# One set of logits for two softmaxes: raw logits kept in DRAM, shifted by GpSimd, transposed by TensorE

## Chip, cores, metric

One Trainium2 chip, one of its cores. The metric is the device time of one launch in microseconds; lower is better. Engines are called TensorE (PE in the profile, PEld for its weight loads), VectorE (DVE), ScalarE (ACT), GpSimd (POOL) and SyncE (SP, which only issues DMAs). "q" behind an engine's name is its sequencer.

## What is computed

Eight batch elements of 256 tokens x 128 channels go through four residual layers, all in float32. The change touches the third layer's mixture of slots (64 experts with 32 slots each, 2048 columns). Both softmaxes are taken of the same logits: D over the 32 slots of an expert, C over the 64 experts of a slot.

```python
logits = (jnp.einsum('tzd,ed->tze', x, phi_w) + phi_b).reshape(t, z, n, p)   # t=8, z=256, n=64, p=32
D = jax.nn.softmax(logits, axis=3)
C = jax.nn.softmax(logits, axis=2)
X_tilde = jnp.einsum('tznp,tzd->npd', D, x)          # summed over all batch elements
X_tilde = tanh(layer_norm(clip(X_tilde)))
Y_tilde = jnp.einsum('npd,ndH->npH', X_tilde, expert_w) + expert_b[:, None, :]
Y = jnp.einsum('tznp,npH->tzH', C, Y_tilde)
```

X_tilde needs D of all eight elements before Y of the first can be made: so the layer has a join in its middle. The layer before it (a mixture of MLPs and skills) makes u, the x of these lines. The fourth layer is a linear attention input, 16-head attention and a routed feed-forward.

## The kernel before

The kernel works in stages. Stage A holds layer 1 and half of layer 2. Stage B holds, for each batch element b, the end of layer 2 (BC, Z, LN, ZN, ZT, X2), the skills (SG, SU, UC, UT) and the D side of the slots (LG, MT, SH, XT, MC). Then comes the join (JC, JR, JB, JT, JX, JN, JM, JA: norm, tanh, the experts' products). Stage D holds the C side (CL, CSA, CSB, CSUM, REC, CN, Y, X3) and layer 4 (S, V, Q, K, RQ, RK, QM, MX, NM, TS, AV, AVT, SAT, WO, X5, G3, GE, FF, SO, RT, FIN, OUT, ST).

The order on each engine is written out by hand as a string of steps, NAME.b, in ORDER_BD (stages B to D) and ORDER_A. Each engine runs its own string in that order, so a step whose semaphore has not come holds all that stand behind it on its engine. Steps of several batch elements are mixed, so that stage B of b+1 runs beside that of b. PSUM is two halves of four banks: low (the skills, later CL and layer 4) and high (the logits, later the attention scores).

D side, per batch element, in eight steps of 512 columns (four of 1024: half h of the columns and half k of the tokens, each in two parts c). TensorE makes LG in a bank of high (L1021, f32, and L1022, the bias in three bf16 parts). VectorE reduces it over slots (L1822), splits the negated maxima in two bf16 parts (L1824, L1826), and reduces over experts (L1827). TensorE transposes the maxima (MT, L1029), ScalarE copies them (L1406), TensorE adds them to the bank with a selection matrix (SH, L1033), and ScalarE takes exp of it (L1411). VectorE sums (L1834) and scales (L1838); XT (L1046) multiplies by u and VectorE adds to xacc (L1847). MC joins the maxima over experts (L1852) and leaves them transposed in mcR.

C side, per batch element. TensorE makes the logits again, transposed, in eight steps CL of two 128-column tiles (L1104), with maxima and bias from mcR and selPx (L1105). ScalarE takes exp into eC (L1438). GpSimd adds quarters of eC (CSA L2118, CSB L2123), VectorE adds the rest (CSUM, L1894 to L1898), TensorE folds it over partitions (L1111), VectorE takes the reciprocal (REC, L1901) and scales eC in four steps (CN, L1907). Y (L1118) multiplies by the experts' outputs in four steps. X3 (L1910) adds it to x.

Other names: W and WA on GpSimd make weights of layer 4 (L2098, L2101), RSZ the norm's power for ZN (L2080, L2082); JR the same for the join. L1766 to L1773 on VectorE pick the tokens of layer 2 and scale the mask that BC.0 waits for. EWA and EWB load expert weights, EBD the biases and layer 4's weights (18 loads).

## Time and profile before

| | us |
|---|---|
| median of 3 runs | 1195.12 |
| lowest, highest | 1194.73, 1200.56 |
| the profiled execution | 1194.49 |
| its span, first to last instruction | 1192.6 |

| engine | busy us | share of the span | instructions |
|---|---|---|---|
| TensorE | 1032.1 | 87% | 6734 |
| VectorE | 765.5 | 64% | 1829 |
| ScalarE | 518.0 | 43% | 836 |
| GpSimd | 158.1 | 13% | 166 |

The rows below are of the profiled execution, which took 1.9 us more than its span. Busy times of TensorE are those of a pipelined engine: a listed duration holds the way through the array, and the next instruction starts before it ends, so starts are to be compared for its rate. A share over the whole span is an average over stages with different limits.

### The profile page before, as it was taken

What the parts mean: (1) busy time and instruction counts of PE and PEld (TensorE: products, weight loads), DVE (VectorE), ACT (ScalarE), POOL (GpSimd) and SP (SyncE); (2) the same over time, 40 slices, a digit from 0 to 9 for tenths busy, and PEclk for the clock granted to TensorE, in tenths of its full rate; (3) what the DMA queues carried; (4) which work ended last, traced back from release to release, by engine and by line L of the source; (5) the groups of instructions that cost most, each with busy time, mean ns of one, the idle gap of its engine ahead of it and who ended that gap; (6) DMA issues with size and microseconds to landing.
All of it is one profiled execution on the core that took longest, in us unless ns stands there. A gap on an engine that the chain in (4) does not pass through costs nothing.

```text
span 1192.6 us, 18208 instructions
## 1 busy us (share of the span) xinstructions
PE 1032.1 (87%) x6734; PEld 765.7 (64%) x6760; DVE 765.5 (64%) x1829; ACT 518.0 (43%) x836; POOL 158.1 (13%) x166
## 2 busy tenths in 40 slices
PE   3989999998648899999999953788999999998755
PEld 2878888886436667776766733566666666666432
DVE  4565555554574678888888777536567676676432
ACT  1245445435322554465557312235455536543510
POOL 1120110100307300000000004201212022011000
PEclk9999999999768999999999987999999999999976
DMA  8010000000300221001300003000000000000000
GB/s 319 2 28 15 14 15 14 14 14 2 124 0 1 85 93 54 17 38 53 124 1 1 1 1 107 1 1 1 1 6 1 6 1 5 6 1 6 5 5 5
DMA packets 11800, 35.39 MB, mean 30 GB/s; under 512 B 2570, under 2 KB 5818, under 8 KB 10944
## 3 DMA queue, kind: packets, MB, share of 16 engines
q1 hardware_dynamic: 10464, 33.14, 7.8%
q8 instruction: 54, 0.88, 0.3%
q10 hardware_dynamic: 1152, 1.05, 0.3%
q14 instruction: 34, 0.28, 0.1%
q0 software_dynamic: 96, 0.04, 0.0%
HBM read 33.16 MB, written 1.06 MB: 29 GB/s over the span
## 4 chain that ended last, share of the span: by engine, by line
PE 58%; issue 18%; DVE 15%; DVEq 4%; ACT 2%; POOL 1%; POOLq 1%; another core or an unknown queue 0%; ACTq 0%
PE ps L1118 5%; PE ps L1104 5%; PE ps L836 5%; PE ps L1001 3%; PE ps L1046 3%; PE ps L1258 3%; PE ps L1179 3%; PE ps L1159 2%; DVE arena L1822 2%; PE ps L1197 2%; PE ps L870 2%; PE ps L1021 2%; PE ps L846 2%; PE ps L882 2%; PE ps L994 2%
## 5 line engine op out<-in xcount | busy, mean ns | idle before, releaser
L1926 DVE TENSOR_REDUCE arena<-ps 128x8 f32<-128x2048 f32 x32 | 73.3, 2291 | 37.3 <-PE ps L1159 37.3
L1465 ACT ACTIVATE arena<-ps 128x2048 f32<-128x2048 f32 x32 | 60.1, 1879 | 57.5 <-PE ps L1183 57.5
L1104 PE MATMUL ps<-uR,arena 128*128 128x256 f32 x256 | 74.6, 386 | 0.1
L1258 PE MATMUL ps<-arena 128*128 128x512 f32 x128 | 68.2, 657 | 5.5 <-DVE xacc L2000 4.4
L1021 PE MATMUL ps<-arena,uR 128*128 128x512 f32 x128 | 67.7, 610 | 3.5 <-ACT arena L1411 3.0
L1046 PE MATMUL ps<-arena 128*128 128x128 f32 x512 | 64.9, 281 | 6.7 <-DVE arena L1838 5.0
L1046 PEld LDWEIGHTS ps<-arena 128*128 128x128 f32 x512 | 62.4, 196 | 12.1 <-issue 7.9
L1118 PE MATMUL ps<-arena 128*128 128x256 f32 x256 | 63.9, 395 | 6.6 <-DVE arena L1907 3.7
L1438 ACT ACTIVATE arena<-ps 128x512 f32<-128x512 f32 x64 | 38.0, 598 | 60.5 <-PE ps L1105 54.1
L1118 PEld LDWEIGHTS ps<-arena 128*128 128x128 f32 x256 | 47.9, 194 | 20.0 <-issue 9.6
L836 PE MATMUL ps<-arena 128*128 128x256 f32 x256 | 58.0, 384 | 0.0
L994 PE MATMUL ps<-x2R,arena 128*128 128x256 f32 x192 | 52.0, 394 | 5.6 <-DVE arena L1813 5.4
L1822 DVE TENSOR_REDUCE arena<-ps 128x16 f32<-128x512 f32 x64 | 44.3, 692 | 17.7 <-remote 7.9
L836 PEld LDWEIGHTS ps<-arena 128*128 128x128 f32 x256 | 49.2, 193 | 7.3
L986 PE MATMUL ps<-x2R,arena 128*128 128x256 f32 x192 | 51.0, 388 | 0.9 <-ACT arena L1392 0.4
L1411 ACT ACTIVATE arena<-ps 128x512 f32<-128x512 f32 x64 | 38.2, 598 | 29.7 <-PE ps L1033 28.5
L1104 PEld LDWEIGHTS ps<-uR,arena 128*128 128x128 f32 x256 | 39.6, 190 | 16.7 <-issue 5.2
L994 PEld LDWEIGHTS ps<-x2R,arena 128*128 128x128 f32 x192 | 35.0, 193 | 18.3 <-DVE arena L1813 12.9
L1001 PE MATMUL ps<-arena 128*128 128x256 f32 x192 | 43.3, 380 | 3.5 <-DVE arena L1813 3.5
L1258 PEld LDWEIGHTS ps<-arena 128*128 128x128 f32 x128 | 23.5, 201 | 33.5 <-issue 20.0
L1179 PE MATMUL ps<-arena,x1C 32*128 32x256 f32 x512 | 41.3, 409 | 3.4 <-ACT arena L1465 3.3
L1827 DVE TENSOR_REDUCE arena<-ps 128x32 f32<-128x512 f32 x64 | 43.8, 684 | 0.2 <-issue 0.2
(381 smaller groups left out, 2355.5 us busy)
## 6 DMA issues: line engine op xcount, KB each, us to landing
arena<-in_skills SPq DMA_DIRECT2D x16, 768.0 KB, 5.7
arena<-in_expert_w SPq DMA_DIRECT2D x2, 2048.0 KB, 8.3
arena<-in_l_experts SPq DMA_DIRECT2D x8, 386.5 KB, 3.1
arena<-in_consts_b SPq DMA_DIRECT2D x1, 1152.0 KB, 9.5
x2R<-in_x ACTq DMA_DIRECT2D x8, 128.0 KB, 6.5
arena<-in_L_w SPq DMA_DIRECT2D x2, 512.0 KB, 12.1
arena<-in_phiC SPq DMA_DIRECT2D x1, 1024.0 KB, 12.6
arena<-in_expert_b SPq DMA_DIRECT2D x1, 1024.0 KB, 4.9
```

The source lines that it names most:

```text
L836: last = mm(mid[:, j * T:(j + 1) * T], w0[w][:, e, :], S8a[u][:, e, :], start=e == 0, stop=e == E - 1)
L994: last = mm(low[:, 3, j * T:(j + 1) * T], w[:, 4 + 2 * h + j, :], x2R[:, b, :], start=True, stop=True)
L1001: last = mm(low[:, 2, 0:T], w[:, 8 + j, :], H3[u][:, 4 * m + j, :], start=m == 0 and j == 0, stop=m == 2 and j == 3)
L1021: mm(high[:, c, :], uR[:, b, k * P:(k + 1) * P], phiC[:, col:col + 512], start=True, stop=False)
L1046: last = mm(high[:, 2, t * P:(t + 1) * P], eD[h][:, k, col:col + P], uT[u][:, k, :], start=k == 0, stop=k == 1)
L1104: mm(o, phiC[:, st_ * P:(st_ + 1) * P], uR[:, b, :], start=True, stop=False)
L1118: last = mm(low[:, 1, 0:T], ytl[:, t, :], eC[u][:, t, :], start=t == 0, stop=t == ST - 1)
L1179: mm(scores[:, c, h * T:(h + 1) * T], kR[u][row, t * P:(t + 1) * P], qm[u][row, g, :], start=True, stop=False)
L1258: last = mm(low[:, 3, :], pm[:, 2 + j, k * P:(k + 1) * P], w2e[:, j, c * 512:(c + 1) * 512], start=j == 0, stop=j == 1)
L1465: av(pexp[:, t, gp].rearrange("p c h t -> p (c h t)"), scores[:, :, :].rearrange("p c t -> p (c t)"), ACT.Exp, scale=SCALE3).then_inc(s.sc ...
L1822: V.tensor_reduce(nmd, lg, X, ALU.max, negate=True)
L1926: V.tensor_reduce(nm[:, k, :, 2 * gp:2 * gp + 2], scores[:, :, :].rearrange("p c (h t) -> p c h t", h=2), X, ALU.max, negate=True).then_in ...
```

## The change

The logits are made once per batch element. LG writes to one of three banks of high in turn, ScalarE copies it raw to SBUF (LC, new; raw[j], four tiles of 1024 columns, where stage B's hid was), and VectorE takes both maxima from there, four steps LG instead of eight (nmd over slots, nmc over experts). GpSimd adds the slot maxima (DS, new), ScalarE takes exp in place (SH, four of 1024). MT, the SH products and MC's transpose go; MC is one minimum. SyncE stores each raw tile to DRAM (KP, 512 KB each).

For the C side SyncE reads 2 MB per element back (BACK: tokens on partitions, double buffer cT). GpSimd adds the expert maxima (CM, two of 2048), ScalarE takes exp (CE, two of 2048), VectorE sums over the 64 experts in one reduction per half (CB, reading 32 words apart), takes the reciprocal of 64 sums and spreads it over 256 columns (REC). TensorE transposes these (CR) and the 16 tiles of both halves (TC, eight steps of four transposes in place of CL), VectorE copies CR's result (RC) and scales each TC step from PSUM into eC (CN, eight steps of 512), which is now one buffer; Y waits for all CN. CSA, CSB, CSUM, selPx, mcR and three constants go. EWA, EWB and EBD wait for other things, and ORDER_BD is written anew for all engines. The arena grows from 35396 to 37240 words.

In the diff a line of three dots stands where lines are left out, most of the removed ones among them.

```diff
 ORDER_BD = {
     "SP": """
-    LOAD.0 LOAD.1 LOAD.2 EWA.0 LOAD.3 LOAD.4 LOAD.5 LOAD.6 EWB.0 LOAD.7 EBD.0 ST.0 ST.1 ST.2 ST.3 ST.4 ST.5 ST.6
-    ST.7""",
+    LOAD.0 LOAD.1 LOAD.2 KP0.0 KP1.0 KP2.0 KP3.0 LOAD.3 KP0.1 KP1.1 KP2.1 KP3.1 LOAD.4 KP0.2 KP1.2 KP2.2 KP3.2 LOAD.5
+    KP0.3 KP1.3 KP2.3 KP3.3 LOAD.6 KP0.4 KP1.4 KP2.4 KP3.4 LOAD.7 KP0.5 KP1.5 KP2.5 KP3.5 EWA.0 KP0.6 KP1.6 KP2.6
+    KP3.6 BACK.0 KP0.7 KP1.7 KP2.7 KP3.7 EWB.0 BACK.1 EBD.0 BACK.2 BACK.3 BACK.4 BACK.5 ST.0 BACK.6 ST.1 BACK.7 ST.2
+    ST.3 ST.4 ST.5 ST.6 ST.7""",
     "ACT": """
...
+    UC.7 SH3.6 UT.7 LC0.7 LC1.7 LC2.7 CE0.0 LC3.7 LC4.7 SH0.7 LC5.7 LC6.7 CE1.0 LC7.7 SH1.7 SH2.7 SH3.7 CE0.1 CE1.1
+    JT0.0 JT1.0 JN0.0 JN1.0 CE0.2 CE1.2 S.0 V.0 NM.0 CE0.3 TS0.0 CE1.3 TS1.0 S.1 TS2.0 V.1 AV0.0 TS3.0 AV1.0 CE0.4
...
     "DVE": """
...
+    SH2.6 SH3.6 LG0.7 XT1.6 CB0.0 SH0.7 XT2.6 LG1.7 XT3.6 LG2.7 LG3.7 SH1.7 MC.7 CB1.0 XT0.7 XT1.7 SH2.7 SH3.7 REC.0
+    XT2.7 JC0.0 RC.0 XT3.7 JC1.0 JB0.0 CN0.0 CN1.0 JB1.0 CN2.0 CN3.0 CN4.0 CN5.0 CB0.1 CN6.0 CN7.0 CB1.1 REC.1 JA0.0
+    JA1.0 CB0.2 CB1.2 X3.0 RQ.0 RC.1 RK.0 CN0.1 CN1.1 MX0.0 CN2.1 CN3.1 MX1.0 CN4.1 CN5.1 MX2.0 CN6.1 CN7.1 MX3.0 NM.0
+    REC.2 CB0.3 X3.1 CB1.3 RQ.1 RK.1 RC.2 REC.3 CN0.2 CN1.2 MX0.1 CN2.2 CN3.2 MX1.1 CN4.2 CN5.2 MX2.1 CN6.2 CN7.2
...
     "POOL": """
-    W.0 WA.0 W.1 RSZ.0 WA.1 W.2 WA.2 W.3 RSZ.1 WA.3 W.4 WA.4 W.5 WA.5 RSZ.2 W.6 WA.6 W.7 WA.7 RSZ.3 RSZ.4 RSZ.5
...
+    W.0 W.1 WA.1 W.2 WA.2 W.3 WA.3 W.4 WA.4 W.5 WA.5 W.6 WA.6 W.7 WA.7 RSZ.0 RSZ.1 RSZ.2 DS0.0 DS1.0 RSZ.3 DS2.0 DS3.0
+    DS0.1 DS1.1 DS2.1 DS3.1 DS0.2 RSZ.4 DS1.2 DS2.2 DS3.2 DS0.3 DS1.3 RSZ.5 DS2.3 DS3.3 RSZ.6 DS0.4 DS1.4 DS2.4 RSZ.7
+    DS3.4 DS0.5 DS1.5 DS2.5 DS3.5 DS0.6 DS1.6 DS2.6 DS3.6 CM0.0 DS0.7 CM1.0 DS1.7 DS2.7 DS3.7 CM0.1 CM1.1 JR0.0 VZ.0
+    JR1.0 CM0.2 CM1.2 QM.0 CM0.3 CM1.3 QM.1 CM0.4 CM1.4 RS1.0 QM.2 CM0.5 CM1.5 RS1.1 QM.3 RS2.0 CM0.6 CM1.6 RS1.2
+    RS2.1 QM.4 CM0.7 CM1.7 RS1.3 QM.5 RS2.2 RS1.4 QM.6 RS2.3 RS1.5 QM.7 RS2.4 RS1.6 RS2.5 RS1.7 RS2.6 RS2.7""",
...
+                for j in range(4):
+                    if n == f"KP{j}":
+                        sp.wait_ge(s.raw_copied, at(b, 8, 2 * j + 1))
+                        sp.dma_start(raw_d[b, j // 2, j % 2], raw[j]).then_inc(kept[j], 16)
...
+                if n == "EWB":
+                    sp.wait_ge(s.max_ready, 8 * NB)
+                    sp.wait_ge(s.shifted, 4 * NB)
+                    for j in range(4):
+                        sp.wait_ge(kept[j], 16 * NB)
+                    sp.dma_start(ew_c[1], A["expert_w"][1]).then_inc(s.ew_loaded, 16)
...
+                if n == "BACK":
+                    if b == 0:
+                        sp.wait_ge(s.uC_mm, NB)
+                    if b == 1:
+                        sp.wait_ge(s.lg_mm, 8 * NB)
+                    if b >= 2:
+                        sp.wait_ge(s.tc_mm, at(b - 2, 9, 8))
+                    for j in range(4):
+                        sp.wait_ge(kept[j], 16 * at(b))
+                    for k in range(K):
+                        sp.dma_start(cT[u][k].rearrange("p (h c) -> p h c", h=2),
+                                     raw_d[b, :, k].rearrange("h p c -> p h c")).then_inc(raw_back[u], 16)
...
+                        if i >= 3:
+                            pe.wait_ge(s.raw_copied, i - 2)
                         col = h * HALF + c * 512
...
+                        bank = high[:, LG_BANK[i % 3], :]
+                        mm(bank, uR[:, b, k * P:(k + 1) * P], phiC[:, col:col + 512], start=True, stop=False)
+                        mm(bank, ones_rows, phib3[:, col:col + 512], start=False, stop=True).then_inc(s.lg_mm, 1)
...
+                if n == "CR":
+                    pe.wait_ge(s.csum_ready, at(b, 3, 2))
+                    if b == 0:
+                        pe.wait_ge(s.zn_ready, NB)
+                        pe.wait_ge(s.zn_aff, NB)
+                    else:
+                        pe.wait_ge(s.rope_done, at(b - 1, 4, 0))
+                    for k in range(K):
+                        last = tr(low[:, 0, k * P:(k + 1) * P], rsum[:, k * P:(k + 1) * P], ident)
+                    last.then_inc(s.tc_mm, 1)
+                if n[:2] == "TC":
                     a = int(n[2:])
                     if a == 0:
...
+                        pe.wait_ge(s.eC_ready, at(b, 9, 0))
+                        pe.wait_ge(s.c_exp, at(b, 2, 1))
+                    elif a == 1:
                         if b > 0:
...
+                            pe.wait_ge(s.rope_done, at(b - 1, 4, 2))
                     else:
...
+                        pe.wait_ge(s.eC_ready, at(b, 9, a - 1))
                     for t in range(2):
...
+                        for k in range(K):
+                            st_ = 2 * a + t
+                            last = tr(low[:, a % 2, t * T + k * P:t * T + (k + 1) * P], cT[u][k][:, st_ * P:(st_ + 1) * P], ident)
+                    last.then_inc(s.tc_mm, 1)
...
+                    if n == f"LC{st_}":
+                        act.wait_ge(s.lg_mm, at(b, 8, st_))
+                        if c == 0:
+                            if b == 0:
+                                act.wait_ge(s.z_mm, at(j))
+                            else:
+                                act.wait_ge(s.max_ready, at(b - 1, 8, 2 * j + 1))
+                                act.wait_ge(s.shifted, at(b - 1, 4, j))
+                                act.wait_ge(kept[j], 16 * b)
+                        av(raw[j][:, c * 512:(c + 1) * 512], high[:, LG_BANK[i % 3], :], ACT.Copy).then_inc(s.raw_copied, 1)
+                for j in range(4):
+                    if n == f"SH{j}":
+                        act.wait_ge(s.shifted, at(b, 4, j))
+                        av(eD[j // 2][:, j % 2, :], eD[j // 2][:, j % 2, :], ACT.Exp).then_inc(s.eD_ready, 1)
...
+                    if n == f"CE{k}":
+                        act.wait_ge(s.c_shifted, at(b, 2, k))
+                        av(cT[u][k], cT[u][k], ACT.Exp).then_inc(s.c_exp, 1)
...
+                    if n == f"LG{j}":
                         dr()
...
+                        dve.wait_ge(s.raw_copied, at(b, 8, 2 * j + 1))
+                        if 4 * b + j >= 2:
+                            dve.wait_ge(s.shifted, 4 * b + j - 1)
+                        lg = raw[j].rearrange("p (n q) -> p n q", q=PSLOT)
+                        V.tensor_reduce(nmd[j % 2], lg, X, ALU.max, negate=True).then_inc(s.max_ready, 1)
+                        V.tensor_reduce(nmc[:, k, h, :], lg.rearrange("p n q -> p q n"), X, ALU.max,
+                                        negate=True).then_inc(s.max_ready, 1)
...
+                    V.tensor_tensor(mcA[:, b, :].rearrange("p (k q) -> p k q", k=K), nmc[:, :, 0, :], nmc[:, :, 1, :],
+                                    ALU.min).then_inc(s.mc_ready, 1)
...
+                    if n == f"CB{k}":
+                        dr()
+                        dve.wait_ge(s.c_exp, at(b, 2, k))
+                        V.reduce_sum(csum[:, k * PSLOT:(k + 1) * PSLOT], cT[u][k].rearrange("p (n q) -> p q n", q=PSLOT),
+                                     X).then_inc(s.csum_ready, 1)
                 if n == "REC":
...
+                    dr()
+                    V.reciprocal(csum, csum)
+                    dr()
+                    if b > 0:
+                        dve.wait_ge(s.tc_mm, at(b - 1, 9, 0))
+                    V.tensor_copy(rsum.rearrange("p (k r q) -> p k r q", k=K, r=4),
+                                  csum.rearrange("p (k q) -> p k q", k=K).unsqueeze(2).to_broadcast([P, K, 4, PSLOT])).then_inc(s.csum_ready, 1)
+                if n == "RC":
+                    dve.wait_ge(s.tc_mm, at(b, 9, 0))
+                    V.tensor_copy(rC, low[:, 0, 0:T]).then_inc(s.eC_ready, 1)
+                if n[:2] == "CN":
+                    a = int(n[2:])
+                    dve.wait_ge(s.tc_mm, at(b, 9, a + 1))
+                    if a == 0:
                         dr()
...
+                        if b == 0:
+                            dve.wait_ge(s.uC_mm, NB)
+                        else:
+                            dve.wait_ge(s.Y_mm, at(b - 1))
+                    V.tensor_tensor(eC[:, 2 * a:2 * a + 2, :], low[:, a % 2, :].rearrange("p (t c) -> p t c", t=2),
+                                    rC.unsqueeze(1).to_broadcast([P, 2, T]), ALU.mult).then_inc(s.eC_ready, 1)
...
+                    if n == f"DS{j}":
+                        pool.wait_ge(s.max_ready, at(b, 8, 2 * j))
+                        if b > 0:
+                            pool.wait_ge(s.xt_mm, at(b - 1, 4, 2 * h + 1))
+                        tile = [P, 32, PSLOT]
+                        G.tensor_tensor(eD[h][:, k, :].rearrange("p (n q) -> p n q", q=PSLOT),
+                                        raw[j].rearrange("p (n q) -> p n q", q=PSLOT),
+                                        nmd[j % 2].unsqueeze(2).to_broadcast(tile), ALU.add).then_inc(s.shifted, 1)
...
+                    if n == f"CM{k}":
+                        pool.wait_ge(raw_back[u], 32 * (b // 2 + 1))
+                        pool.wait_ge(s.mc_ready, at(b))
+                        c = cT[u][k].rearrange("p (n q) -> p n q", q=PSLOT)
+                        G.tensor_tensor(c, c, mcA[:, b, k * PSLOT:(k + 1) * PSLOT].unsqueeze(1).to_broadcast([P, NSLOT, PSLOT]),
+                                        ALU.add).then_inc(s.c_shifted, 1)
```

## Rows read from the trace of the kernel before

**Rows 1.** Busy table: stretch, length, busy us (PE, PEld, DVE, ACT, POOL), PEclk, DMA

```profile
460.00:660.00 200.00, 189.90 (x1000) 143.06 (x1016) 171.18 (x321) 113.16 (x173) 3.37 (x7) 1.00 0.12 43
...
660.00:717.00 57.00, 43.24 (x233) 30.06 (x236) 42.54 (x76) 15.63 (x35) 0.30 (x2) 0.94 0.00 1
...
826.00:1070.00 244.00, 241.76 (x1955) 162.15 (x1954) 162.99 (x293) 131.04 (x187) 41.48 (x33) 1.00 0.01 3
```

**Rows 2.** Chain of waits from 742 us on: start us, us, what

```profile
825.80 1.83 PE ps L1118 x8
...
1070.15 1.73 PE ps L1118 x8
```

**Rows 3.** Groups by form, stage B: line, operation, count | busy us, mean ns | idle

```profile
L1822 DVE TENSOR_REDUCE arena<-ps 128x16 f32<-128x512 f32 x64 | 44.3, 692 | 17.7 <-remote 7.9 <-PE ps L1022 5.0 <-issue 1.0
...
L1824 DVE CAST arena<-arena 128x16 bf16<-128x16 f32 x64 | 12.4, 193 | 5.0 <-issue 0.4
...
L1827 DVE TENSOR_REDUCE arena<-ps 128x32 f32<-128x512 f32 x64 | 43.8, 684 | 0.2 <-issue 0.2
...
L1834 DVE TENSOR_REDUCE arena<-arena 128x32 f32<-128x1024 f32 x32 | 38.7, 1211 | 0.6 <-ACT arena L1411 0.5
...
L1852 DVE TENSOR_REDUCE arena<-arena 128x64 f32<-128x256 f32 x8 | 4.8, 596 | 0.8
```

**Rows 4.** Order of time on TensorE: start us, us, engine, line, operation

```profile
894.23 0.60 PE L1207 MATMUL ps<-cst,arena 128*128 128x128 f32 x4
...
912.18 0.59 PE L1104 MATMUL ps<-uR,arena 128*128 128x256 f32 x2
...
912.62 0.28 PE L1105 MATMUL ps<-mcR,selPx 67*128 67x256 bf16 x1
...
912.73 0.60 PE L1104 MATMUL ps<-uR,arena 128*128 128x256 f32 x2
```

**Rows 5.** Groups by form, stage D

```profile
L1901 DVE RECIPROCAL y1C<-ps 128x256 f32<-128x256 f32 x8 | 14.0, 1754 | 3.7 <-PE ps L1111 3.6
...
L1907 DVE TENSOR_TENSOR arena<-arena,y1C 128x1024 f32<-128x1024 f32 x32 | 38.4, 1220 | 0.6
...
L1894 DVE TENSOR_TENSOR arena<-w3raw,arena 128x1024 f32<-128x1024 f32 x8 | 9.8, 1225 | 4.7 <-ACT arena L1438 4.5 <-POOL w3raw L2123 0.2
...
L1465 ACT ACTIVATE arena<-ps 128x2048 f32<-128x2048 f32 x32 | 60.1, 1879 | 57.5 <-PE ps L1183 57.5
...
L1438 ACT ACTIVATE arena<-ps 128x512 f32<-128x512 f32 x64 | 38.0, 598 | 60.5 <-PE ps L1105 54.1 <-PE ps L1001 6.1
```

**Rows 6.** Order of time on GpSimd and VectorE where both work

```profile
328.60 1.91 POOL L2098 TENSOR_TENSOR arena<-w3raw,condc 128x1024 f32<-128x1024 f32 x1
...
328.81 1.98 DVE L1754 TENSOR_TENSOR arena<-arena 128x256 f32<-128x256 f32 x1
...
330.87 0.43 DVE L1756 TENSOR_TENSOR arena<-arena 128x256 f32<-128x256 f32 x1
...
375.78 2.35 POOL L2101 TENSOR_TENSOR wb<-wb,arena 128x1024 f32<-128x1024 f32 x1 [0.16 <-issue]
...
377.48 0.75 DVE L1813 SCALAR_TENSOR_TENSOR arena<-ps,wsel,arena 128x512 f32<-128x512 f32 x1 [0.65 <-PE ps L994]
...
393.27 2.15 DVE L1805 TENSOR_TENSOR x2R<-x2R,sqC 128x256 f32<-128x256 f32 x1 [3.98 <-ACT sqC L1385]
```

**Rows 7.** Order of time on VectorE at the start of stage B

```profile
350.85 0.29 DVE L1770 TENSOR_SCALAR arena<-arena 128x256 f32<-128x256 f32 x1
...
351.23 2.19 DVE L1773 TENSOR_SCALAR arena<-arena,cst 128x256 bf16<-128x256 f32 x8
```

**Rows 8.** Order of time on VectorE around the join

```profile
716.73 0.82 DVE L1864 TENSOR_SCALAR xacc<-xacc 128x1024 f32<-128x1024 f32 x1
...
749.05 0.42 DVE L1910 TENSOR_TENSOR x2R<-x2R,ps 128x256 f32<-128x256 f32 x1 [7.35 <-PE ps L1118]
```

**Rows 9.** DMA issues: count, KB each, median us to landing

```profile
arena<-in_expert_w SPq DMA_DIRECT2D x2, 2048.0 KB, 8.3
```

386 lines of the change are left out of this document (122 added, 264 removed).

## Prediction

> **What bounds the kernel now.** I read the busy table by stretch first, then the grouped instructions, then the order of time on single engines. [rows 1] In the steady part of the middle stage (460 to 660 us, called stage B) TensorE is busy 189.9 us of 200 and VectorE 171.2 of 200, with 321 VectorE instructions and their short gaps filling most of the rest: two engines are full together. From 660 to 717 us, where the last batches have no TensorE work left to overlap, VectorE is busy 42.5 of 57 us. In the last stage (stage D, 826 to 1070) TensorE is busy 241.8 of 244 and VectorE 163.0: TensorE bounds it. [rows 2] give the first quarter of the Y product of batches 2 and 7 (825.80 and 1070.15), so five batches take 244.35 us, 48.9 each. GpSimd works 41 us of those 244 and 3.4 us of the 200 in stage B: it is the free engine that the change loads.
>
> **The change, part by part.**
>
> Stage B, TensorE. Per batch eight MT transposes and eight SH products go. A bf16 product of 256 columns advances the queue by 0.11 us (912.62 to 912.73 [rows 4]), so SH of 512 costs 0.22, eight are 1.8 us; an MT, of 64 columns, is below the 0.11 of that row, some 0.5 for eight. TensorE saves some 2.3 us of 39 per batch, 18 in all.
>
> Stage B, VectorE. Now each half tile costs two reductions, 0.692 and 0.684 us, and two short conversions near 0.19 [rows 3]: 64 x 1.75 = 112 us. After it each of 32 tiles of 1024 columns costs a contiguous maximum, 1.211 (as L1834 does), and one over the experts, which steps 32 words in SBUF. The nearest row for that is L1852: 256 elements, same step, 0.598 us. L1822 and L1834 differ by 0.52 us for 512 elements, so contiguous reading costs 1.01 ns an element and 0.17 us for the instruction; L1852 leaves 1.66 ns an element. The maximum over experts is then 0.17 + 1024 x 1.66 ns = 1.87 us, and 32 x 3.08 = 99 us: 13 less. MC falls from 0.6 + two conversions to one short operation: 6 less. Fewer instructions in a chain save about 4 us of gaps. Together -23. Bounds for the strided maximum: 1.21 (contiguous) to 1.87, since both are rows.
>
> What it adds there: the two strided sums of batch 0 are put before the join of the stages, at 0.17 + 2048 x 1.66 ns = 3.57 us each, and a reciprocal and a copy of 64 to 256 elements: +8.
>
> GpSimd's holds. DS adds four GpSimd operations of 1024 elements per batch. Rows for such operations run from 1.91 to 2.35 us [rows 6]. They hold VectorE: at 328.81 a 256-element operation that takes 0.43 elsewhere (330.87) took 1.98, ending 0.28 after GpSimd's at 330.51. At 377.48 an operation with one input in PSUM ran 0.75 us inside a GpSimd operation (375.78 to 378.13) as ever. So those with both inputs in SBUF wait. Stage B has six of these per batch (four SH multiplies, X2, MC). GpSimd would be busy 9.4 us of 38, a quarter; a hold met at random costs half its 2.35: 48 x 0.25 x 1.2 = 14 us. GpSimd also waits on VectorE and DS falls mostly beside the reductions, so I take +10 (0 to 28, all meeting one). The Trainium skill, "SBUF — State Buffer", section "SBUF: two separate sides", says that a GpSimd operation and a VectorE one with two SBUF inputs (or in a two-port mode) exclude each other for the whole instruction, and others are not held. The two rows agree, and by that rule the strided maxima, with one input, run free and the sum stays as below. No row has such a maximum inside a GpSimd operation; were it held too, all 32 x 2.35 = 75 us of DS could fall on VectorE, and the sum would end 65 later.
>
> Stage B together: -23 + 8 + 10 = -5, between TensorE's own -18 and +13.
>
> The end of stage B. SP loads BACK.0 (2 MB) only after the last UC; GpSimd has CM0.0 in front of DS0.7 in its queue, so all of batch 7's DS wait behind that load and a 2048-element CM. A 2 MB load lands in 8.3 us [rows 9]; CM is two of the 1.91 to 2.35 us operations, 4.2. DS0.7 could start some 5 us after UC.7 and starts after 12.5; VectorE has 3 to 4 us of other work there. +4 (0 to 8).
>
> The start of stage B. Today's order stops GpSimd after W.1 until statistics come; the new one runs all W and WA at once, 13 operations of about 2.2 us, to about 360 us. VectorE still has three two-input or two-port operations before its top-k loop, then the nine scalings of L1770 and L1773 that TensorE's BC.0 waits for [rows 7]. Three holds of about 1.9 net are 5.6 us; the loop itself (one data input) ends at 356 then, and its followers meet the last W: 3 more. Back comes what those W cost later, as at 393.27 (2.15 for a 0.43 operation [rows 6]): -3. Net +6 (0 to 12).
>
> The join. JR0.0 (the norm's power, GpSimd) now stands behind CM0.1 and CM1.1, and JT0.0 (tanh, ScalarE) behind CE1.1; both need BACK.1, issued behind a 2 MB EWB that itself waits for the last DS. Two such loads are 14 to 16 us from the last DS, the two CM 8.4. X3.0 on VectorE stands behind CB1.2, which needs BACK.2, issued after the 18 loads of EBD. Today JC.0 to X3.0 is 32.7 us (716.73 to 749.05, and its 0.42 [rows 8]). Followed through the new queues, counted from JC.0: TC.0 ends near 17, BACK.2 lands at 25.5, CM 30 and 34, CE 36, CB1.2 40, X3.0 after it: +7 (0 to 14, the lower end where the loads land early).
>
> Stage D, TensorE. A CL step is two pairs of 0.44 + 0.11 (912.18, 912.62, 912.73): 1.10 us. A TC step is four f32 128x128 transposes: listed with 0.60 us for four, and as a listed duration overruns the advance by 0.17 (0.28 for 0.11 at 912.62), 0.11 each, 0.44 [rows 4]. 8 x 0.66 = 5.3 us per batch less; CSUM's product is replaced by two transposes, about 0.2 less.
>
> Stage D, VectorE. Out: CSUM (1.22 and, by size, 0.69 and 0.43), REC 1.75, four CN of 1.22 [rows 5]: 9.0. In: two sums 7.1, reciprocal and copies 1.2, eight CN from PSUM at 0.7 (as the 0.75 of 377.48 for 512 columns): 13.9. 163.0/5 = 32.6 becomes 37.5, with gaps about 40.5. CM holds GpSimd's side 8.4 us per batch instead of CSA and CSB's 4.3; few D operations have two SBUF inputs, and the four CN and CSUM that had leave: +1. TensorE needs 48.9 - 5.5 = 43.4 if nothing else moved. With VectorE at 41.5 in order beside it I expect 45.5, -3.4 x 6 batch steps = -20 (-32 if TensorE alone sets it, +4 if VectorE does at 49.5). ScalarE and the DMA queues hide: CE is 2 x 1.88 against CL's 8 x 0.6 [rows 5], and 2 MB in and 2 MB out per batch are 17 us of DMA in 39 or 48; without that cover each would show as waits of CM or LC.
>
> Sum on the profiled execution, 1194.49 us (span 1192.6): +6 - 5 + 4 + 7 - 20 = -8, so 1186. The median of the runs shown is 1195.12, 0.6 more.
>
> **The rivals.**
>
> TensorE keeps its whole saving: the holds and the join cost little, B gives 18, D 32, the start 6 back: 1194.5 - 44 = 1150. For it: TensorE is the fullest engine in both stages. Against: VectorE is as full in B, and grows in D.
>
> Nothing shows: D gives half (-10), the queues' new positions eat it: 1189 to 1201. For it: four waits on BACK lie on chains that nothing covers.
>
> Slower: GpSimd holds VectorE. Where DS and the six two-input operations fall together always (one waits for the other's result through ScalarE, so they keep step), B loses 30 instead of 10 and D's holds take 5 us per batch: VectorE 45, step 48: -1 x 6. +6 + 15 + 4 + 7 - 6 = +26, 1220. It decides from about 18 us of holds in B with D at -12. For it: 1.98 for 0.43. Against: the operations with PSUM inputs run free.
>
> **How the numbers follow.** Forecast 0.42 (its own range 1176 to 1196), TensorE alone 0.18, nothing 0.15, slower by holds 0.25. 0.5% is 6 us, about what a measurement of this kernel can tell from none. Faster than 1189: all of the first rival and most of the forecast's lower part, 0.48; within 1189 to 1201: 0.23; slower 0.29. Two in ten left out: 1153 to 1216.
>
> **What would show it.** The sums over experts at 3.6 us and the maxima at 1.9 (2.3 and 1.2 would refute L1852 as the model). TC steps 0.44 apart. Y's quarters 45.5 us apart. X2, SH's multiply and MC lengthened where DS runs. BC.0 starting 9 us later. VectorE idle before CB0.0, CB1.2. Wrong: steps of D at 48 or more, or a join longer by over 14 us.

## The result, and the profile after

The changed kernel takes 1228.61 us (median of 4, 1223.07 to 1236.55), the kernel before beside it 1197.05. The ratio is 1.0266 with a 95% interval of 1.0202 to 1.0331: 2 to 3% slower, where 1186 was forecast. The profiled execution took 1236.55 us with a span of 1234.8, the longest of the four; stretches below are of it, so their sum, 42.2 us, is some 11 more than the difference of the medians. Of run e8 below, one of five executions, the profiled one (1162.48 us), was in a slower state of the chip, so its time here is the median of the other four.

First where the time lies. From the order of time on TensorE I took when the first instruction of a step starts (end: the last instruction of the span). The last column is the fastest kernel of the experiments (e14 below: the changed kernel with its steps in another order and one GpSimd instruction cut in four).

| from, to | before, us | after, us | difference | forecast | e14, us |
|---|---|---|---|---|---|
| start to UC.0 | 386.9 | 390.9 | +4.0 | +6 | 377.8 |
| UC.0 to UC.7 (stage B) | 270.6 | 290.9 | +20.3 | -5 | 253.5 |
| UC.7 to the end of XT.7 | 58.4 | 68.9 | +10.5 | +4 | 62.7 |
| end of XT.7 to Y.0 | 25.9 | 25.4 | -0.5 | | 21.8 |
| Y.0 to OUT.0 | 143.7 | 155.0 | +11.3 | +7 with the row above | 136.0 |
| OUT.0 to the end | 307.0 | 303.7 | -3.3 | -20 | 277.3 |
| whole span (rows rounded singly) | 1192.6 | 1234.8 | +42.2 | -8 | 1129.0 |

The busy table of the changed kernel, in the columns and for the stretches of [rows 1]; the last line is its own stage B:

```profile
460.00:660.00 200.00, 173.94 (x862) 134.98 (x872) 155.67 (x181) 86.99 (x115) 39.85 (x27) 0.94 0.23 90
660.00:717.00 57.00, 42.95 (x200) 30.19 (x201) 47.17 (x43) 23.26 (x32) 20.98 (x9) 0.95 0.28 111
826.00:1070.00 244.00, 214.39 (x1775) 147.06 (x1776) 178.54 (x294) 94.39 (x131) 48.37 (x29) 0.93 0.10 37
390.90:681.80 290.90, 255.07 (x1238) 194.20 (x1251) 217.06 (x256) 126.85 (x172) 55.03 (x38) 0.95 0.23 91
```

and stage B of the kernel before (386.90 on) and of e14 (377.80 on):

```profile
386.90:657.50 270.60, 254.04 (x1323) 189.82 (x1345) 223.48 (x419) 152.86 (x232) 14.66 (x17) 1.00 0.14 51
```

```profile
377.80:631.30 253.50, 241.71 (x1247) 183.40 (x1247) 216.33 (x255) 141.80 (x185) 75.24 (x47) 0.99 0.28 102
```

What to see: in [rows 1] TensorE and VectorE were both nearly full; after, neither is. In stage B TensorE idles 290.9 - 255.1 = 35.8 us instead of 16.6 (+19.2), and its mean granted clock is 0.95 instead of 1.00, which by estimate is 0.05 x 290.9 = 14.5 us of full-speed work not granted (somewhat less, since a part of the low clock fell in idle time). Without those 14.5 its work is some 240.6 us against 254.0 (-13.4): the work did shrink. +19.2 + 14.5 - 13.4 = 20.3. VectorE has 6.4 us less work and also waits more. The e14 line has the same instructions, GpSimd's cut one apart, with TensorE idle 11.8 us: the saving is there once the order lets it be.

The waits of stage B that engines spent on each other, after (engine, line, waited for: us, times, longest; L997 is SU, L1797 the instruction of VectorE it needs, L1037 is XT, L1828 VectorE's addition of it):

```profile
PEld ps L997 <- DVE arena L1797: 20.5, 19, 4.0
DVE xacc L1828 <- PE ps L1037: 20.3, 11, 3.8
...
PE ps L997 <- DVE arena L1797: 11.7, 9, 3.6
...
PE ps L1037 <- DVE xacc L1828: 9.1, 3, 4.5
```

TensorE waits for VectorE and VectorE for TensorE, in turn. In the kernel before the first three of these pairs are 12.5, 7.3 and 5.4 us in stage B and the fourth does not occur there; in e14 the four are 12.7, 2.9, 5.7 and 0.7 us.

The groups that answer to [rows 3] and [rows 5], by form:

```profile
L1806 DVE TENSOR_REDUCE arena<-arena 128x32 f32<-128x1024 f32 x32 | 39.0, 1220 | 11.8 <-ACT arena L1398 7.9 <-issue 3.4 <-POOL arena L2063 0.3
L1807 DVE TENSOR_REDUCE arena<-arena 128x32 f32<-128x1024 f32 x32 | 61.8, 1931 | 0.0
...
L1868 DVE TENSOR_REDUCE arena<-arena 128x32 f32<-128x2048 f32 x16 | 58.8, 3676 | 33.9 <-ACT arena L1422 32.9
...
L1890 DVE TENSOR_TENSOR arena<-ps,y1C 128x512 f32<-128x512 f32 x64 | 41.5, 685 | 6.2 <-PE ps L1093 5.0
...
L2063 POOL TENSOR_TENSOR arena<-arena 128x1024 f32<-128x1024 f32 x32 | 60.9, 1904 | 213.1 <-DVE arena L1806 186.1 <-PE ps L1037 27.0
...
L2102 POOL TENSOR_TENSOR arena<-arena,mcA 128x2048 f32<-128x2048 f32 x16 | 64.5, 4053 | 140.7 <-DMA arena<-raw_scratch 140.7
```

These are the two maxima of LG, the sum CB, the scaling CN, and GpSimd's DS and CM. Each lies within 4% of the forecast's size (1.21, 1.87, 3.57, 0.7; DS at the lower end of 1.91 to 2.35; CM 4.2). New is the last figure of L1868: VectorE stood still 32.9 us in front of the sums, waiting for ScalarE's exp of them.

The Y product, first quarter of batches 2 and 7 (order of time on TensorE), for [rows 2]:

```profile
850.23 1.57 PE L1102 MATMUL ps<-arena 128*128 128x256 f32 x6
...
1091.37 1.90 PE L1102 MATMUL ps<-arena 128*128 128x256 f32 x8
```

241.1 us for five batches, 48.2 each against 48.9: of TensorE's 5.5 us per batch, 0.7 appeared.

### The profile page after: what moved, and what is told of

Its sections match the earlier page's. It is cut to its first block, busy times and chain, and to the rows that moved or that the text cites. A ratio compares the mean times of both kernels' runs of the same rounds, so it can differ in the third digit from the quotient of the medians.

```text
span 1234.8 us, 17278 instructions
## 1 busy us (share of the span) xinstructions
PE 1003.0 (81%) x6473; PEld 756.4 (61%) x6488; DVE 804.1 (65%) x1661; ACT 462.8 (37%) x700; POOL 239.2 (19%) x192
## 4 chain that ended last, share of the span: by engine, by line
PE 37%; issue 33%; DVE 11%; POOL 8%; DVEq 4%; ACT 4%; POOLq 3%; ACTq 0%; another core or an unknown queue 0%
PE ps L840 5%; POOL arena L2102 4%; PE ps L997 2%; PE ps L1037 2%; PE ps L989 2%; PE ps L886 2%; PE ps L874 2%; PE ps L1242 2%; DVE arena L1815 2%; PE ps L850 2%; PE ps L897 2%; POOLq L2078 2%; DVE arena L1868 1%; PE ps L1102 1%; DVE arena L1819 1%
## 5 line engine op out<-in xcount | busy, mean ns | idle before, releaser
L1037 PE MATMUL ps<-arena 128*128 128x128 f32 x512 | 76.0, 311 | 44.2 <-DVE arena L1819 25.3
L1037 PEld LDWEIGHTS ps<-arena 128*128 128x128 f32 x512 | 72.2, 222 | 52.4 <-issue 35.6
L2063 POOL TENSOR_TENSOR arena<-arena 128x1024 f32<-128x1024 f32 x32 | 60.9, 1904 | 213.1 <-DVE arena L1806 186.1
L2102 POOL TENSOR_TENSOR arena<-arena,mcA 128x2048 f32<-128x2048 f32 x16 | 64.5, 4053 | 140.7 <-DMA arena<-raw_scratch 140.7
L1910 DVE TENSOR_REDUCE arena<-ps 128x8 f32<-128x2048 f32 x32 | 73.2, 2288 | 13.8 <-PE ps L1143 13.4
L1868 DVE TENSOR_REDUCE arena<-arena 128x32 f32<-128x2048 f32 x16 | 58.8, 3676 | 33.9 <-ACT arena L1422 32.9
L1102 PE MATMUL ps<-arena 128*128 128x256 f32 x256 | 63.0, 394 | 5.9 <-DVE arena L1855 5.8
L997 PE MATMUL ps<-x2R,arena 128*128 128x256 f32 x192 | 54.2, 407 | 12.9 <-DVE arena L1797 12.5
L1422 ACT ACTIVATE arena<-arena 128x2048 f32<-128x2048 f32 x16 | 30.6, 1910 | 86.3 <-POOL arena L2102 86.2
L1807 DVE TENSOR_REDUCE arena<-arena 128x32 f32<-128x1024 f32 x32 | 61.8, 1931 | 0.0
L1102 PEld LDWEIGHTS ps<-arena 128*128 128x128 f32 x256 | 49.4, 199 | 16.4 <-issue 8.9
L840 PE MATMUL ps<-arena 128*128 128x256 f32 x256 | 59.4, 391 | 0.0
L1402 ACT ACTIVATE arena<-arena 128x1024 f32<-128x1024 f32 x32 | 33.8, 1057 | 60.2 <-POOL arena L2063 60.0
L840 PEld LDWEIGHTS ps<-arena 128*128 128x128 f32 x256 | 50.2, 197 | 7.6
L1376 ACT ACTIVATE arena<-ps 128x512 f32<-128x512 f32 x48 | 28.7, 598 | 66.4 <-PE ps L989 66.1
L1398 ACT ACTIVATE arena<-ps 128x512 f32<-128x512 f32 x64 | 37.8, 595 | 42.2 <-PE ps L1025 26.4
L997 PEld LDWEIGHTS ps<-x2R,arena 128*128 128x128 f32 x192 | 35.7, 198 | 28.0 <-DVE arena L1797 22.8
L1163 PE MATMUL ps<-arena,x1C 32*128 32x256 f32 x512 | 43.7, 429 | 10.3 <-ACT arena L1448 7.0
## 6 DMA issues: line engine op xcount, KB each, us to landing
arena<-in_L_w SPq DMA_DIRECT2D x2, 512.0 KB, 10.5
```

Of the source, the lines that this page charges most:

```text
L840: last = mm(mid[:, j * T:(j + 1) * T], w0[w][:, e, :], S8a[u][:, e, :], start=e == 0, stop=e == E - 1)
L997: last = mm(low[:, 3, j * T:(j + 1) * T], w[:, 4 + 2 * h + j, :], x2R[:, b, :], start=True, stop=True)
L1037: last = mm(high[:, 2, t * P:(t + 1) * P], eD[h][:, k, col:col + P], uT[u][:, k, :], start=k == 0, stop=k == 1)
L1102: last = mm(low[:, 1, 0:T], ytl[:, t, :], eC[:, t, :], start=t == 0, stop=t == ST - 1)
L1807: V.tensor_reduce(nmc[:, k, h, :], lg.rearrange("p n q -> p q n"), X, ALU.max, negate=True).then_inc(s.max_ready, 1)
L1868: V.reduce_sum(csum[:, k * PSLOT:(k + 1) * PSLOT], cT[u][k].rearrange("p (n q) -> p q n", q=PSLOT), X).then_inc(s.csum_ready, 1)
```

## The experiments

All times are medians; "to before" is the ratio to the kernel before on the same chip, with its 95% interval. The changed kernel itself is 1.0266 (1.0202 to 1.0331).

| run | what | us | to before |
|---|---|---|---|
| e1 | maximum over a quarter of the experts | 1217.89 | 1.0219 (1.0179 to 1.0259) |
| e2 | sum over a quarter of the experts | 1217.44 | 1.0186 (1.0165 to 1.0207) |
| e3 | DS on a quarter of the columns | 1226.01 | 1.0279 (1.0249 to 1.0308) |
| e4 | raw logits of one element stored | 1229.71 | 1.0282 (1.0255 to 1.0309) |
| e6 | sums later in VectorE's queue | 1238.85 | 1.0344 (1.0288 to 1.0400) |
| e7 | steps of the D side reordered | 1187.55 | 0.9931 (0.9909 to 0.9953) |
| e8 | all steps of stages B to D reordered | 1148.35 | 0.9601 (0.9560 to 0.9643) |
| e9 | the kernel before, reordered likewise | 1176.48 | 0.9827 (0.9789 to 0.9865) |
| e10 | e8 by a second search | 1155.15 | 0.9680 (0.9663 to 0.9696) |
| e11 | e9 by the second search | 1198.22 | 1.0034 (1.0021 to 1.0046) |
| e12 | e6, with CM in four pieces | 1214.05 | 1.0172 (1.0153 to 1.0191) |
| e13 | halving on GpSimd, then VectorE's sum | 1249.39 | 1.0467 (1.0433 to 1.0502) |
| e14 | e8, with CM in four pieces | 1132.02 | 0.9472 (0.9426 to 0.9518) |
| e15 | after, with CM in four pieces | 1230.86 | 1.0287 (1.0219 to 1.0355) |

### Is it the new work itself? (e1 to e4)

e1 takes three quarters of the strided maximum away:

```diff
-  V.tensor_reduce(nmc[:, k, h, :], lg.rearrange("p n q -> p q n"), X, ALU.max, negate=True)
+  V.tensor_reduce(nmc[:, k, h, :], lg[:, 0:8, :].rearrange("p n q -> p q n"), X, ALU.max, negate=True)
...
```

> The changed kernel, with the maximum over the experts taken over 8 of a tile's 32 experts (three quarters of that reduction are left out). The changed kernel takes 1228.6. In its trace such a reduction takes 1.93 us; with a quarter of the elements it should take about 0.6, so VectorE loses 32 x 1.33 = 43 us of work, 40 of them before the join. If VectorE's amount of work sets the time of stage B, 1190 to 1200. If stage B is set by the chain from one engine to the next (slot maximum, GpSimd's addition, exp, sum) and by gaps in fixed orders, only what stands in a chain comes back: 1212 to 1222. If GpSimd holds VectorE, 1228: this operation has one input and was not lengthened.

```profile
L1807 DVE TENSOR_REDUCE arena<-arena 128x32 f32<-128x256 f32 x32 | 18.9, 589 | 0.0
```

and its stage B, in the columns of [rows 1]:

```profile
389.80:664.40 274.60, 243.65 (x1237) 186.17 (x1250) 187.41 (x256) 126.41 (x171) 55.02 (x38) 0.99 0.25 96
```

VectorE lost 61.8 - 18.9 = 43 us of work, 30 of them in the stage in which it was thought to bound, and the kernel 11 us by the medians (6 by the ratios). Stage B took 274.6 us in this one trace, where it took 290.8 to 290.9 in those of the changed kernel and of e2, e4, e6, e13 and e15, which leave it alone. So VectorE's work has a part in it; but TensorE's idle time fell by 4.9 us only (35.8 to 31.0), most of the rest is its clock (0.99 instead of 0.95), and the four waits above still are 16.7, 18.0, 9.6 and 8.8 us. With 36 us less VectorE work in it than the kernel before, the stage is still 4 us longer than there. e2 does the same to the sum:

```diff
-  V.reduce_sum(csum[...], cT[u][k].rearrange("p (n q) -> p q n", q=PSLOT), X)
+  V.reduce_sum(csum[...], cT[u][k][:, 0:16 * PSLOT].rearrange("p (n q) -> p q n", q=PSLOT), X)
```

> The changed kernel, with the sum over the experts taken over 16 of 64 (three quarters of that reduction are left out). In the trace of the changed kernel it takes 3.67 us; a quarter should take 1.0, so VectorE loses 16 x 2.65 = 42 us of work, 5 of them ahead of the join. If the single long reduction is what costs stage D its gain, 1195 to 1205. If stage D is set by waits (read back, GpSimd, exp, with this sum standing ahead of other work in VectorE's queue), the sum waits as long as before and only its own length goes where it stands in that chain: 1212 to 1222.

```profile
L1868 DVE TENSOR_REDUCE arena<-arena 128x32 f32<-128x512 f32 x16 | 16.6, 1039 | 46.7 <-ACT arena L1422 46.1
```

58.8 - 16.6 = 42 us of work went, 10 to 11 us of time. The line shows where a part of the rest is: the wait in front of the sum grew from 32.9 to 46.1 us, since a shorter instruction waits longer for the same exp. In both runs about a quarter of the work taken off VectorE comes back as time, by the medians.

e3 makes GpSimd's shift short in elements 1 to 7, e4 stores element 0 alone and reads that back for all:

```diff
-  tile = [P, 32, PSLOT]
+  w = 32 if b == 0 else 8
+  tile = [P, w, PSLOT]      # and 0:w * PSLOT of eD, raw, 0:w of nmd
```

> The changed kernel, with GpSimd adding the slot maxima to 256 of a tile's 1024 columns in batch elements 1 to 7 (the rest of the addition is left out). In the trace an addition takes 1.90 us; a quarter should take 0.6. 28 x 1.3 = 36 us of GpSimd's time go, and each tile's chain from maximum to sum is 1.3 us shorter. If the chain through GpSimd sets stage B, 1205 to 1216. If VectorE's work sets it, 1226 to 1229. If GpSimd holds VectorE, the lengthened VectorE instructions of the trace (1.3 us in all between 353 and 660 us, 5.2 more around the join, most of these by the other GpSimd addition) bound the gain at 3: 1225 to 1229.

```diff
-  sp.dma_start(raw_d[b, j // 2, j % 2], raw[j]).then_inc(kept[j], 16)
+  if b == 0:
+      sp.dma_start(raw_d[b, j // 2, j % 2], raw[j]).then_inc(kept[j], 16)
...
-                   raw_d[b, :, k].rearrange("h p c -> p h c")).then_inc(raw_back[u], 16)
+                   raw_d[0, :, k].rearrange("h p c -> p h c")).then_inc(raw_back[u], 16)
...
```

> The changed kernel, with only batch element 0's raw logits stored, and read back for every element (28 of the 32 stores are left out). ScalarE's raw copies then wait for no store of the element before. In the trace these copies wait 14.5 us in 8 places between 460 and 680 us for something outside the engines. If these waits set stage B, 1210 to 1218; if they are covered by other work, 1226 to 1229.

```profile
L2064 POOL TENSOR_TENSOR arena<-arena 128x256 f32<-128x256 f32 x28 | 17.2, 617 | 218.4 <-DVE arena L1806 189.2 <-PE ps L1037 29.2
```

DS fell from 1.90 to 0.62 us and nothing moved that can be told from noise: GpSimd waits 189 us for VectorE's maxima anyway, and its presence beside VectorE is not what slows stage B. The 28 stores (14 of 16 MB) cost nothing that can be measured; the interval of either run covers the changed kernel's ratio.

### Is it the wait in front of the sum? (e6)

The sums of element 2 block VectorE before X3.0 (order of time on VectorE, after; L1894 is X3):

```profile
781.08 7.44 DVE L1868 TENSOR_REDUCE arena<-arena 128x32 f32<-128x2048 f32 x2 [5.16 <-ACT arena L1422]
788.43 0.41 DVE L1894 TENSOR_TENSOR x2R<-x2R,ps 128x256 f32<-128x256 f32 x1
```

So I moved the sums and reciprocals of stage D behind work that was ready (one stretch of VectorE's string):

```diff
-JA1.0 CB0.2 CB1.2 X3.0 RQ.0 RC.1 RK.0 CN0.1 CN1.1 MX0.0 CN2.1 CN3.1 MX1.0 CN4.1 CN5.1 MX2.0 CN6.1 CN7.1 MX3.0 NM.0
+JA1.0 CB1.1 REC.1 X3.0 RQ.0 RC.1 RK.0 CN0.1 CN1.1 MX0.0 CN2.1 CN3.1 MX1.0 CN4.1 CN5.1 MX2.0 CN6.1 CN7.1 MX3.0 CB0.2 NM.0 CB1.2
```

> The changed kernel, all of it, with only the sums over the experts and their reciprocals (CB, REC) moved in VectorE's queue, most of them later (CB0.2 and CB1.2 from ahead of X3.0 to 16 places further, CB1.6 and CB1.7 by 20); nothing else differs. The changed kernel takes 1228.6. Theory 'position': a sum that waits for read back, GpSimd and exp holds what stands behind it; VectorE stood idle 32.9 us in six such places. Then 1210 to 1220. Theory 'work': the sum costs its 3.67 us wherever it stands: 1226 to 1230. If the gaps also set the TensorE clock, more than the gaps comes back: below 1210.

It became 10 us slower (9 by the ratios), against the theory. What took the place of the wait (e6, order of time on GpSimd and VectorE; L2104 is CM, L1917 and L1919 are two small operations of NM inside SBUF):

```profile
807.75 8.26 POOL L2104 TENSOR_TENSOR arena<-arena,mcA 128x2048 f32<-128x2048 f32 x2 [17.98 <-DMA arena<-raw_scratch]
...
808.68 3.61 DVE L1917 CAST arena<-arena 128x32 bf16<-128x32 f32 x1
...
812.36 3.70 DVE L1919 TENSOR_TENSOR arena<-arena 128x32 bf16<-128x32 f32 x1
```

The cast takes 0.18 us in the median of its eight. Where the wait had been, VectorE now had operations inside SBUF to do, and met CM with them. A VectorE instruction that is lengthened while GpSimd works is called held. I counted the holds in each trace: every VectorE instruction that overlaps a GpSimd one, less the median of the same line and shape without overlap. From 775 to 1100 us they are 7.9 us after and 22.5 in e6; from 660 to 775, 5.6 and 9.0.

### Is it the order? (e7, e8, e9)

On TensorE of the changed kernel, UC.5 starts at 589.66 and UC.6 at 647.66: 58 us apart where a batch takes 41.6 on average, with eleven LG steps and five XT of elements 4 and 5 between them in TensorE's string; from UC.4 to UC.5 it is 39.7 us, with seven LG and five XT. Steps were moved within their engine's queue only, the instructions left as they are; the order was found by a search that played queues, waits and the durations of this trace; the times told are the chip's. e7 moves nine kinds of step (LG, LC, DS, SH, XT, MC and W, WA, RSZ), of TensorE 115 and of VectorE 70 steps by more than one place (here, as in the edits after it, one stretch of a string):

```diff
 VectorE
-SU0.4 XT1.2 MC.2 SH3.2 SU1.4 BC0.5 LG0.3 BC1.5 SU2.4 SU3.4 SH0.3 SU4.4 LG1.3
+SU0.4 LG3.2 SU1.4 BC0.5 BC1.5 XT0.2 SU2.4 XT1.2 MC.2 SH3.2 LG0.3 SU3.4 XT2.2 SU4.4 SH0.3 LG1.3
 TensorE
-UC.4 ZT.5 XT3.2 UT.4 BC0.6 LG6.3 SG0.5
+UC.4 ZT.5 UT.4 LG0.4 BC0.6 XT0.3 SG0.5
```

> The changed kernel, all of it, with only the steps of the logits' D side (LG, LC, DS, SH, XT, MC) and GpSimd's weights (W, WA, RSZ) moved within their engines' queues; 115 of TensorE's 596 steps and 70 of VectorE's 502 move by more than one place, and nothing is added or left out. Position: stage B lost 20 us against the kernel before although no VectorE instruction there was longer than alone; it lost them by waits in fixed orders, and 20 to 40 come back: 1190 to 1208. Work: it stays at 1224 to 1230.

It came out 2 us below the range given for positions. Its stage B:

```profile
380.60:638.50 257.90, 241.62 (x1232) 185.13 (x1250) 219.59 (x254) 139.15 (x183) 84.60 (x51) 0.99 0.27 103
```

Against the changed kernel's 290.9 us that is 33.0 less, with 2.5 us more VectorE work in the stretch: TensorE idles 16.3 us instead of 35.8, and its clock is 0.99 instead of 0.95. UC.0 starts 10.3 us earlier as well.

e8 lets every step of stages B to D move (TensorE 336 of 596, VectorE 273 of 502):

```diff
 VectorE
-ZN.7 SU0.6 MC.4 LG0.5 SU1.6 SH3.4 LG1.5 SU2.6 XT0.4 XT1.4 SU3.6 XT2.4 LG2.5 SU4.6 SH0.5 SH1.5 XT3.4 SU5.6
+LG3.4 BC1.7 SU2.6 MC.4 SH3.4 XT0.4 LG0.5 LN.7 SU3.6 XT1.4 LG1.5 SU4.6 ZN.7 XT2.4 SU5.6 LG2.5 XT3.4 SH0.5
```

> The changed kernel, with all steps of stages B to D free to move within their engines' queues, the same instructions. The order was searched with durations and semaphores of the changed kernel's trace, at full TensorE clock and without holds of VectorE by GpSimd. Position: the change saves TensorE 5.3 us per element in stage D and 2.3 in stage B, and this shows when nothing stands behind a wait: 1140 to 1170, so faster than the kernel before. Work: 1215 to 1230. Holds: orders made without regard to them meet them, and the gain stays under half: 1185 to 1200.

e9 is the control, the kernel before by the same search (TensorE 370 of 732, VectorE 175 of 486):

```diff
 VectorE
-LG7.4 SU0.6 MC.4 XT1.4 LG0.5 X2.7 SU1.6 SH3.4 SU2.6 LG1.5 XT2.4 LG2.5 SU3.6
+LG7.4 MC.4 LG0.5 XT1.4 SU0.6 LG1.5 SU1.6 SH3.4 LG2.5 SU2.6 SH0.5 SU3.6 LG3.5
```

> The kernel before, without the change, its steps of stages B to D searched in the same way as for the reordered changed kernel. It tells how much such a search gives where nothing was changed: TensorE is busy 190 of 200 us and 242 of 244 in the two stages, so little can come back there; start, join and tail have gaps. 1168 to 1185. If the search gives the kernel before as much as the changed one (over 50 us), the changed kernel's loss is not one of positions.

With no instruction more or less, the changed kernel loses 41 us by the first edit and 80 by the second; the same treatment takes 18 to 21 off the kernel before, and next to none of that in the two full stages: e9's stage B is 269.9 us (270.6 before), and its quarters of Y stand 242.4 / 5 = 48.5 us apart (48.9). In the searched orders the change is 28 us faster (1148.4 against 1176.5), in the given ones 32 slower. The loss was in the order.

### Would a better search do more? (e10, e11)

A second search also counted holds and half clock. e10 starts from the changed kernel, e11 from the kernel before:

```diff
 VectorE, e10
-LG0.5 SU1.6 SH3.4 LG1.5 SU2.6 XT0.4 XT1.4 SU3.6 XT2.4 LG2.5 SU4.6 SH0.5 SH1.5 XT3.4
+LG0.5 SU3.6 XT1.4 LG1.5 SU4.6 XT2.4 SU5.6 LG2.5 XT3.4 X2.7 SH0.5 SH1.5
 VectorE, e11
-XT1.4 LG0.5 X2.7 SU1.6 SH3.4 SU2.6 LG1.5 XT2.4 LG2.5 SU3.6
+XT1.4 SU1.6 LG0.5 SH3.4 LG1.5 SU2.6 LG2.5 SH0.5 XT2.4 SU3.6
```

> The changed kernel, the same instructions, all steps of stages B to D reordered once more: this search also counted that a GpSimd operation and a VectorE one with two SBUF inputs (or a copy or conversion within SBUF) exclude each other, and that TensorE runs at half clock after a stretch in which it stood idle, both as the traces show them. The first reordering takes 1150, with 16 us of lengthened VectorE instructions between 775 and 1100 us and 7 around the join. If holds and half clock are what is left of the loss, 1125 to 1142, with lengthened instructions under 12 us between 775 and 1100. If the order of waits was all, 1148 to 1152.

> The kernel before, without the change, searched in the same second way. The first search gave 1176. If the change is worth what its saved TensorE time says (5.3 us per element in stage D, 2.3 in B, some 44 over the kernel, less what VectorE gains), this stays 25 to 45 above the changed kernel searched alike: 1160 to 1172. If both come out within 10 us of each other, the change itself is worth nothing and only the search is.

Both missed their times: e10 is 7 us behind e8, e11 4 us slower than its start. Searched alike, though, the changed kernel is again the faster one, by 43 us (1155.2 against 1198.2), within the 25 to 45 that were expected. A searched order is good to some 2% here, and a difference of that size between two of them is no finding. The 80 us of e8 are larger.

### The holds, and the part that gives the change its name (e12, e13)

e12 is e6 with CM cut in four, so that a piece takes 1.15 us in the mean where CM takes 4.05:

```diff
-  c = cT[u][k].rearrange("p (n q) -> p n q", q=PSLOT)
-  G.tensor_tensor(c, c, mcA[...].unsqueeze(1).to_broadcast([P, NSLOT, PSLOT]), ALU.add).then_inc(s.c_shifted, 1)
+  for part in range(4):
+      c = cT[u][k][:, part * 512:(part + 1) * 512].rearrange("p (n q) -> p n q", q=PSLOT)
+      last = G.tensor_tensor(c, c, mcA[...].unsqueeze(1).to_broadcast([P, 16, PSLOT]), ALU.add)
+  last.then_inc(s.c_shifted, 1)
```

> The kernel with the sums over the experts moved later (1238.9, against 1228.6 of the changed kernel), and GpSimd's addition of the expert maxima (CM) in four pieces of 512 columns in place of one of 2048, so that VectorE gets in between. With the sums later 22.5 us of VectorE's instructions between 775 and 1100 us were lengthened (7.9 in the changed kernel), nearly all small ones that met a CM of 3.8 us. If these holds took the gain of the move and more, the pieces give it back: 1208 to 1220. If they are not the cause, 1234 to 1243. GpSimd's own extra time is three more starts of about 0.1 us per CM.

```profile
L2105 POOL TENSOR_TENSOR arena<-arena,mcA 128x512 f32<-128x512 f32 x64 | 71.6, 1154 | 141.1 <-DMA arena<-raw_scratch 141.1
```

25 us faster than e6 (21 by the ratios) although CM as a whole takes longer (71.6 us against 64.5). Holds fall to 6.3 us from 775 to 1100 and to 0.7 from 660 to 775. So the later sums are worth 15 us against the changed kernel (11 by the ratios), and CM's holds had hidden it.

e13 undoes the named part: GpSimd adds the upper 32 experts to the lower (CH, 1024 elements, behind CM in its queue), and VectorE sums 32. The two hand over through one buffer, csB, so each also waits for the other (waits left out here).

```diff
+  G.tensor_tensor(csB, cT[u][k][:, 0:HALF], cT[u][k][:, HALF:2 * HALF], ALU.add).then_inc(s.c_half, 1)
...
-  V.reduce_sum(csum[...], cT[u][k].rearrange("p (n q) -> p q n", q=PSLOT), X)
+  V.reduce_sum(csum[...], csB.rearrange("p (n q) -> p q n", q=PSLOT), X)
```

> The changed kernel with the part that its name speaks of undone: GpSimd adds the upper 32 experts of a half to the lower 32 (a new step CH, 1024 elements, about 1.9 to 2.4 us), and VectorE sums over 32 experts (about 1.9 us as the maximum over 32) in place of 64 (3.67). CH0 and CH1 stand behind CM1 in GpSimd's queue, for element 1 behind JR1; all other orders are those of the changed kernel. VectorE loses 16 x 1.8 = 29 us of work; with the quarter sum 42 us less gave 8 to 11 us, so by work alone 1221 to 1224. GpSimd's operations lengthen the chain from read back to sum by 2 us or more a half and can hold VectorE: with that 1228 to 1245.

```profile
L2112 POOL TENSOR_TENSOR arena<-arena 128x1024 f32<-128x1024 f32 x16 | 37.6, 2352 | 18.2 <-DVEq L1872 18.2
...
L1870 DVE TENSOR_REDUCE arena<-arena 128x32 f32<-128x1024 f32 x16 | 30.4, 1902 | 75.5 <-POOL arena L2112 75.2
```

21 us slower (24 by the ratios; 4 us above the range expected), though VectorE works 28 us less: its wait in front of the sum grows from 32.9 to 75.2 us. Of these two ways to make the sum, one instruction on VectorE is the better one in this order; it is not what made the changed kernel slow.

### The best of it, and what the pieces do alone (e14, e15)

e14 is e8's order with CM in pieces, e15 the given order with CM in pieces; the edit is e12's.

> The first full reordering of the changed kernel (1150) with GpSimd's addition of the expert maxima (CM) in four pieces of 512 columns. Its trace shows 16.4 us of lengthened VectorE instructions between 775 and 1100 us and 7.2 around the join, most of them small ones or TensorE-bound ones that met a CM of 3.8 us. If these holds lie on the path, 1136 to 1146; if they lie in VectorE's idle time now that the order is loose, 1148 to 1153 (three more starts of 0.1 us per CM).

> The changed kernel with CM in four pieces and nothing else (all orders those of the changed kernel, 1228.6). Pieces and later sums together took 1214.1, later sums alone 1238.9. If a hold by CM costs only where VectorE has come free to meet it, the pieces alone give little: 1222 to 1229 (the trace has 5.2 us of holds at the end of stage B and 7.9 in stage D, and not all of them on the path). If CM's holds were themselves the loss of the changed kernel, 1208 to 1216.

e15 moves nothing and gains nothing, so in the given order the holds of CM cost nothing that shows in the whole. e14 gains 16 us on e8 (15 by the ratios), ends 4 us below the range expected, and is the fastest: 1132.02 us, 5.3% below the kernel before. Its sums, and its clock and load in a stretch of five batches of Y (first quarter of batch 2 to that of 7):

```profile
L1869 DVE TENSOR_REDUCE arena<-arena 128x32 f32<-128x2048 f32 x16 | 59.8, 3737 | 5.5 <-ACT arena L1423 4.3
...
777.20:984.20 207.00, 198.15 (x1746) 137.53 (x1744) 178.70 (x292) 91.09 (x129) 50.77 (x55) 1.00 0.12 43
```

The wait before the sums is 4.3 us instead of 32.9, with the same sums. The quarters stand 207.0 / 5 = 41.4 us apart, TensorE 96% busy at its full 2.4 GHz.

## Why the prediction was wrong, point by point

**The reading of the bound** was right for the kernel before and was carried over wrongly. [rows 1] show two engines full together in stage B. The prediction summed VectorE's terms, -23 + 8 + 10 = -5, and let that stand because it lies between TensorE's own saving (-18) and VectorE's worst case (+13). It did not ask whether the new strings of steps keep the two beside each other. They do not: the waits on each other shown above, +19.2 us of idle TensorE and some 14.5 us at the lower clock. This is the failing step, "Stage B together: -5", measured +20.3; e7, with the same instructions in another order, has -12.7. TensorE's -18 itself was right: e14 has 253.5 us for 270.6, -17.1. From 660 to 717 us the prediction saw no TensorE work left to overlap, but [rows 1] have TensorE busy for 43.2 of those 57 us; no term hung on it.

**The durations** were right, from the nearest rows: the strided maximum 1.93 (1.87 forecast, from L1852 in [rows 3]), the strided sum 3.68 (3.57), CN 0.685 (0.7), CE 1.91 (1.88), CM 4.05 (4.2), DS 1.90 (1.91 to 2.35). Eight transposes of TC are listed with 1.09 us, 0.11 each with the overrun of 0.17 taken off, as forecast.

**GpSimd's holds in stage B** were over-priced: +10 forecast, 1.3 us counted from 353 to 660 us. (The upper end of 28 "all meeting one" is not what its terms give: 48 operations at 1.2 us are 58.) DS starts when the first maximum is done and so runs beside the second, which has one input (order of time, after):

```profile
461.28 1.93 DVE L1807 TENSOR_REDUCE arena<-arena 128x32 f32<-128x1024 f32 x1
...
461.44 1.91 POOL L2063 TENSOR_TENSOR arena<-arena 128x1024 f32<-128x1024 f32 x1 [8.95 <-DVE arena L1806]
```

1.93 us beside DS is its time alone too: the two of the 32 that met no GpSimd instruction took 1.88 and 1.93. This is what no row of before could show, and the bound of 65 us for held maxima falls away. The Trainium skill, "SBUF — State Buffer", section "SBUF: two separate sides", leaves an operation with one SBUF input in no two-port mode unheld, and excludes the others for the whole instruction. The 1.93 agrees, and so do the held ones, 4.69 us for 1.23 below. The rival "slower by holds in B" (1220) has the sign and nearly the size of the result, but not its cause: e3 made DS a third as long for nothing.

**The end of stage B**: +10.5 us, +4 (0 to 8) forecast. The load and CM in front of DS0.7 were foreseen; that the next two CM, of element 1, would hold VectorE's scaling (L1819) on the path was not:

```profile
733.11 9.25 POOL L2102 TENSOR_TENSOR arena<-arena,mcA 128x2048 f32<-128x2048 f32 x2 [13.17 <-DMA arena<-raw_scratch]
...
734.00 4.69 DVE L1819 TENSOR_TENSOR arena<-arena 128x1024 f32<-128x1024 f32 x1
...
740.50 2.94 DVE L1819 TENSOR_TENSOR arena<-arena 128x1024 f32<-128x1024 f32 x1
```

L1819 takes 1.23 us in the median, so the two holds are 3.5 + 1.7 = 5.2 us, ahead of the last XT. In e15, where CM is in pieces, the stretch takes 65.2 us instead of 68.9.

**The start** (+4.0 for +6; BC.0 at 358.9 instead of 351.6, 7.3 us later where 9 was named) and **the join** came out as costed. JC.0 to X3.0 is 750.70 to 788.43, 37.7 us, where it was 32.3 [rows 8]: +5.4 for +7, and VectorE stands behind the sums of element 2 as followed through the queues. Of the 11.3 us that the row "Y.0 to OUT.0" lost, 5.2 lie before X3.0; the other 6.1, from X3.0 to OUT.0, were not priced. There the sum of the next element holds up VectorE again, 7.78 us (order of time on VectorE, after):

```profile
811.93 0.29 DVE L1876 COPY nC<-arena 128x256 f32<-128x256 f32 x1
820.00 3.73 DVE L1868 TENSOR_REDUCE arena<-arena 128x32 f32<-128x2048 f32 x1 [7.78 <-ACT arena L1422]
```

That such waits are all of the 6.1 is argued, not shown.

**Stage D**: -3.3 us from OUT.0 on, -20 forecast, -32 for TensorE alone. The quarters of Y went from 48.9 to 48.2, not 45.5, past the 48 that the prediction named as its sign of being wrong. VectorE's work is 178.5 us of 244, 35.7 a batch where 37.5 was forecast, and does not bound. TensorE is busy 214 of 244 at clock 0.93: again idle and clock, not work. The quarters flatter here: between them lie 80 products of RT, those of five batches, in the kernel before, but 64, those of four, after and in e14. The steps OUT.0 to OUT.4 are the fairer measure: 48.7 us apart before, 49.0 after, so nothing of the saving appeared, and 43.5 in e14, beside the 43.4 that TensorE alone was to give.

**The rival "TensorE keeps its whole saving"** (-44 us) is what the change is worth when both kernels get an order of their own: e14 against e9 is 1132.0 - 1176.5 = -44.5 (-42 by the ratios). A part of that is the cut CM (without it, e8 against e9, it is -28), and two searched orders compare to some 2%, so the equality is partly luck; the sign is not. **"Nothing shows"** had the reason (the queues' new positions eat the gain) with too small a price.

**What stays open**: which single position in the strings costs most. The edits e7 and e8 move many steps at once; that TensorE and VectorE wait in turn is shown, and that another order takes it away, but not by which step.

## What to carry to other kernels

With a fixed order on every engine, a sum of saved busy time is no forecast of saved time: here 43 us off VectorE gave 6 to 11, and the same instructions in another order 80. Before forecasting a change that rewrites the queues, look for each pair of engines that are full together and ask which of them waits for the other in the new strings; and count what lost overlap costs twice, as idle time and as TensorE work at the lower clock. When an experiment that removes a wait makes the kernel slower, look at what runs there now before dropping the theory: e6 was a gain of some 15 us hidden by some 25 us that CM's holds cost.

## What the runs showed of the hardware

- The same 16 products of XT took 3.75 us behind a wait of 4.49 us and 1.95 us ten us later (after, order of time on TensorE): half speed, 1.2 against 2.4 GHz. The mean granted clock was 0.67 from 640 to 650 us, where TensorE was busy 5.9 of 10:

```profile
644.12 3.75 PE L1037 MATMUL ps<-arena 128*128 128x128 f32 x16 [4.49 <-DVE xacc L1828]
...
654.12 1.95 PE L1037 MATMUL ps<-arena 128*128 128x128 f32 x16
...
640.00:650.00 10.00, 5.88 (x22) 5.46 (x23) 9.26 (x11) 1.12 (x3) 0.88 (x1) 0.67 0.68 262
```

- A cast of 32 elements inside SBUF took 3.61 us instead of 0.18 beside a GpSimd instruction of 4.1 us: what is held pays by GpSimd's length, not by its own. Cutting that instruction in four was worth 25 us (e6 to e12) or 16 (e8 to e14), and nothing in the given order (e15), for which 5.6 + 7.9 us of holds were counted after 660 us in the changed kernel.
- A reduction that steps 32 words costs 1.93 us for 1024 elements and 3.68 for 2048, against 1.22 for 1024 contiguous ones: 1.7 ns an element instead of about 1.
